# Third attention of a fused transformer tower: from steps of four token blocks and one head group to steps of two token blocks and both head groups

## The chip, the cores and the metric

The kernel runs on one core of one Trainium2 chip. The metric is the device time of one execution in microseconds (us), as the median of several runs; lower is better. A core has a matmul engine (TensorE, PE in the profile, with its weight loads shown apart as PEld), a vector engine (VectorE, DVE), an engine for activation functions (ScalarE, ACT), a general engine (GpSimd, POOL) and a queue that issues transfers (SyncE, SP). Each engine works through its own list of instructions in order; semaphores order the engines among each other.

## The reference, cut to what matters

The program is a small vision tower: a patch embedding, a feed-forward part, a windowed attention, a second attention with a cosine bias, and then a block whose attention is the third one here, followed by a mixture of eight experts. There are 16 images of 64 tokens each, with 64 features. The part that the change touches is this:

```python
h = _rmsnorm(x, ln1_w)
q = (h @ wq.T).reshape(Bx, Tx, NH, HD).transpose(0, 2, 1, 3)    # 4 heads of 16
k = (h @ wk.T).reshape(Bx, Tx, NKV, HD).transpose(0, 2, 1, 3)   # 2 heads, each for 2 query heads
v = (h @ wv.T).reshape(Bx, Tx, NKV, HD).transpose(0, 2, 1, 3)
q, k = q * cos + _rotate_half(q) * sin, k * cos + _rotate_half(k) * sin
scores = jnp.einsum('bhtd,bhsd->bhts', q, repeat(k)) / jnp.sqrt(jnp.float32(HD))
att = jax.nn.softmax(jnp.where(causal, scores, -1e30), axis=-1)
y = jnp.einsum('bhts,bhsd->bhtd', att, repeat(v)) ...
x = x + y @ wo.T
flat = _rmsnorm(x, ln2_w).reshape(-1, Cx)
...
for e in range(NE):                       # 8 experts, hidden width 170
    hh = jax.nn.silu(flat @ w1[e].T) * (flat @ w3[e].T)
    out = out + weights[:, e:e + 1] * (hh @ w2[e].T)
```

## The kernel before

The tokens of the 16 images are laid on two halves of the 128 partitions, which gives 512 columns. Every stage is worked in two halves of 256 columns, called g = 0 and g = 1. A block w (0 to 7) is one image of each partition half; a half g holds blocks 4g to 4g+3. The order of the work on each engine is written out by hand, so that an instruction waits both for its own semaphores and for all that stands ahead of it on its engine. Matmul results lie in eight PSUM banks of 512 columns (`PS[:, bank, column]`).

The third attention is done in four steps i = 0 to 3. A step i covers the half g = i // 2, all of its four blocks, and one of the two head groups (two heads each). It goes through these functions:

- `scores3(g)` on PE writes the scores of both steps of half g: 16 small matmuls, each of which the profile shows as 2 records (line L596). The first step's scores are in bank 4g, the second's in bank 4g+1. One semaphore increment by 2 at the end releases both steps. `open_scores3` has written the causal mask to all four banks before.
- `shift3(i)` on DVE takes the row maximum (`reduce_max`, L1234) and subtracts it (L1236), from 512 columns of PSUM to the tile `shifted`.
- `turn3(i)` on PE turns `shifted` in four transposes (L606).
- `probabilities3(i)` on ACT takes the exponential (L935).
- `mix3(i)` on PE multiplies by the values in 8 matmuls, 16 records (L620). The values are made by `values3(g)` on PE (L369) and copied by `values3(g)` on ACT (L928).

After the two steps of a half, `divide` on DVE (L1245 and L1247) normalises, `mixed_to_features` on PE turns back (L426), `attended_copy3` on ACT copies (L939), `open3` (L630) and `output3` (L635) on PE make the output projection with the residual, and `squares3` on ACT (L943), `sum_squares3` on DVE (L1409), a power on POOL (L1104), `high_part`, `normalised` and `low_part` on DVE (L1415, L1391, L1397) make the normalised features in two parts. `parts_to_features` on PE (L643) turns them, and `turned_copy` on ACT (L954) and on DVE (L1402) copy them to `xf`.

Then comes the loop over 22 chunks n of the experts' first products. For each n, PE does four matmuls of 512 columns (L707, L708), ACT a SiLU (L973), DVE a product (L1454). PE does `output3(1)`, the output projection of the second half of the third attention, between n = 0 and n = 1. From n = 3 on, the matmuls of n wait for the DVE product of n - 3.

The functions of ACT come in tables; `bring_table(func)` (L794) is a one-column activation that makes the load of a table (ACT_TABLE_LOAD) happen at a place of the program's choice. In the kernel before, the load for SiLU stands right behind `probabilities3(3)`, ahead of `turned_copy(0)` and `attended_copy3(1)`; copies can run with any table.

Of the kernel before, what the change touches and what calls it, by code (L numbers as in the profile page):

```python
# [26 lines left out]
P = 128  # L27
B, C, IMG, PATCH = 16, 3, 128, 16
GRID = IMG // PATCH
N = GRID * GRID  # L30
D = 64
HALF = 64
COLS = B * N * D // P
HC = COLS // 2
# [5 lines left out]
FH, FHD, FKV = 4, 16, 2  # L40
# [46 lines left out]
def build(nc, x0, x0_last, x1, pack_a, pack_b, pack_c, pack_d, pack_e, out):  # L87
    with ExitStack() as ctx:
# [5 lines left out]
        def sem(name):  # L94

            if name not in made:
                made[name] = ctx.enter_context(nc.semaphore(name))
            return made[name]

        idle_bf = sb("idle_bf", [P, 512], BF16)  # L100
        PS = ctx.enter_context(nc.psum_tensor("PS", [P, 8, 512], F32))
# [15 lines left out]
        def c(name):  # L117
            return Cp[:, columns(PACK_C, name)]
# [102 lines left out]
        def const(value):  # L221
            n = CONSTS.index(value)
            return consts[:, n:n + 1]
# [21 lines left out]
        def half(t, g):  # L245
            return t[:, g * HC:(g + 1) * HC]
# [53 lines left out]
        def _(pe):  # L300
            mm, tp = nc.tensor.matmul, nc.tensor.transpose
# [63 lines left out]
            def values(src, w, wide, bank, g):  # L365

                for u in (2 * g, 2 * g + 1):
                    at = (u % 2) * 2 * wide
                    t = mm(PS[:, bank, at:at + 2 * wide], src[:, u * P:(u + 1) * P], w, start=True, stop=True)  # L369
                return t  # L370
# [198 lines left out]
            def values3(g):  # L569
                values(h4f, c("fv"), FKV * FHD, 3 + 4 * g, g).then_inc(sem("v3_mm"), 1)  # L570
# [14 lines left out]
            turned_pair(1, ("fq", "fq_turned"))  # L585


            def scores3(g):

                pe.wait_ge(sem("q3_ready"), g + 1)  # L590
                pe.wait_ge(sem("k3_ready"), g + 1)
                for w in range(4 * g, 4 * g + 4):
                    for hg in range(2):
                        for s in range(2):
                            rows = slice(HALF * s + 32 * hg, HALF * s + 32 * hg + 32)
                            t = mm(PS[HALF * s:HALF * s + HALF, 4 * g + hg, (w % 4) * P:(w % 4 + 1) * P],  # L596
                                   q3[rows, w * N:(w + 1) * N], k3_heads[rows, w].rearrange("q h n -> q (h n)"),
                                   start=False, stop=True, skip_group_check=True)
                t.then_inc(sem("att3_scores"), 2)

            def turn3(i):
                if i >= 2:
                    pe.wait_ge(sem("att3_probs"), i - 1)
                pe.wait_ge(sem("att3_shifted"), i + 1)
                for n in range(4):
                    t = tp(PS[:, 2 + 4 * (i % 2), n * P:(n + 1) * P], shifted[:, i % 2, n * P:(n + 1) * P], ident)  # L606
                t.then_inc(sem("att3_turned"), 1)

            def mix3(i):
                g, ch = i // 2, i % 2  # L610
                if ch == 0:
                    pe.wait_ge(sem("v3_ready"), g + 1)
                pe.wait_ge(sem("att3_probs"), i + 1)
                wide = 2 * (FHD + 1)
                for k in range(2):
                    for s in range(2):
                        for p in range(2):
                            of, w = 2 * k + p, 4 * g + 2 * k + p
                            at = ((2 * k + s) * FKV + ch) * wide
                            t = mm(PS[HALF * p:HALF * p + HALF, 3 + 4 * g, at:at + wide],  # L620
                                   probs[:, i % 2, of * P + s * HALF:of * P + (s + 1) * HALF],
                                   vo3[:, p, (w // 2) * 2 + s, ch].rearrange("q e d -> q (e d)"), start=True, stop=True)
                t.then_inc(sem("att3_mixed"), 1)
# [15 lines left out]
            def parts_to_features(g):  # L639
# [4 lines left out]
                t.then_inc(sem("parts_turned"), 1)  # L644

            scores3(0)
            values3(0)
            values3(1)
            scores3(1)
            turn3(0)  # L650
            turn3(1)
            mix3(0)
            mix3(1)
            turn3(2)
# [32 lines left out]
            for n in range(2 * CH):  # L687
                g, ch = n // CH, n % CH
# [15 lines left out]
                for v in range(2):  # L704
                    at = (2 * ch + v) * P
# [83 lines left out]
        def _(act):  # L789
            f = nc.scalar.activation  # L790

            def bring_table(func):

                f(table_use[:, :], const(1.0), func)  # L794
# [91 lines left out]
            for g in range(2):  # L886
                act.wait_ge(sem("qk2_mm"), g + 1)
                for s in range(2):
                    r = slice(HALF * s, HALF * s + HALF)
                    t = f(q2[r, g * HC:(g + 1) * HC], PS[r, QK2_BANKS[s], 0:HC], ACT.Identity, scale=float(D) ** -0.5, bias=q2_bias[r, :])  # L890
# [9 lines left out]
            for g in range(2):  # L900
# [3 lines left out]
                at = slice(4 * g, 4 * g + 4)  # L904
# [7 lines left out]
            for g in range(2):  # L912
                act.wait_ge(sem("kr_ready"), g + 1)
                for h in range(2):
                    t = f(k3_heads[:, 4 * g:4 * g + 4, h, :], half(kr, g).rearrange("q (w n) -> q w n", n=N),
                          ACT.Copy, scale=c("fhead_mask")[:, h:h + 1])
# [14 lines left out]
            def probabilities3(i):  # L931
                act.wait_ge(sem("att3_turned"), i + 1)
                if i >= 2:
                    act.wait_ge(sem("att3_mixed"), i - 1)
                f(probs[:, i % 2, :], PS[:, 2 + 4 * (i % 2), :], ACT.Exp, scale=scale3).then_inc(sem("att3_probs"), 1)  # L935
# [5 lines left out]
            def squares3(g):  # L941
                act.wait_ge(sem("fo_mm"), g + 1)
                f(squares_eps[:, 4 * g:4 * g + 4, 0:D], PS[:, 4 * g, 0:HC].rearrange("q (t d) -> q t d", d=D), ACT.Square,  # L943
                  scale=float(D) ** -0.5).then_inc(sem("rms2_squared"), 1)
# [7 lines left out]
            def turned_copy(g):  # L952
                act.wait_ge(sem("parts_turned"), g + 1)
                f(xf[:, g, 1, :], PS[:, TURNED_BANKS[1][g], 0:HC], ACT.Copy).then_inc(sem("xf_ready1"), 1)  # L954
# [7 lines left out]
            attended_copy3(0)  # L962
            squares3(0)
            probabilities3(3)
            bring_table(ACT.Silu)
            turned_copy(0)
            attended_copy3(1)

            for n in range(2 * CH):
# [184 lines left out]
        def _(ve):  # L1154
# [27 lines left out]
            def scale(name, g, dst, src, by):  # L1182
                ts = slice(4 * g, 4 * g + 4)
                ve.wait_ge(sem(name + "_rstd"), g + 1)
                return v.tensor_tensor(tiles(dst)[:, ts], tiles(src)[:, ts], by[:, ts].unsqueeze(2).to_broadcast([P, 4, D]),
                                       ALU.mult)
# [41 lines left out]
            def shift(name, rows, n):  # L1228

                ve.wait_ge(sem(name + "_scores"), n + 1)  # L1230
                if n >= 2:
                    ve.wait_ge(sem(name + "_turned"), n - 1)
                tops = top[:, n % 2, :].rearrange("q (b h) -> q b h", b=2)
                v.reduce_max(tops, rows, AX).then_inc(sem(name + "_top"), 1)  # L1234
                ve.wait_ge(sem(name + "_top"), n + 1)
                v.tensor_tensor(shifted[:, n % 2, :].rearrange("q (b h n) -> q b h n", b=2, n=N), rows,  # L1236
                                tops.unsqueeze(3).to_broadcast([P, 2, 4, N]), ALU.subtract)\
                    .then_inc(sem(name + "_shifted"), 1)

            def divide(name, bank, g, heads, size):  # L1240

                ve.wait_ge(sem(name + "_mixed"), (4 if name == "att1" else 2) * (g + 1))
                mix = PS[:, bank, 0:4 * heads * (size + 1)].rearrange("q (w h d) -> q w h d", w=4, h=heads)
                rec = r1[:, 4 * g:4 * g + 4, 0:heads]
                v.reciprocal(rec, mix[:, :, :, size]).then_inc(sem(name + "_recip"), 1)  # L1245
                ve.wait_ge(sem(name + "_recip"), g + 1)
                v.tensor_tensor(on[:, 4 * g:4 * g + 4, :].rearrange("q w (h d) -> q w h d", h=heads), mix[:, :, :, 0:size],  # L1247
                                rec.unsqueeze(3).to_broadcast([P, 4, heads, size]), ALU.mult)\
                    .then_inc(sem(name + "_divided"), 1)
# [132 lines left out]
                v.tensor_tensor(half(kr, g), half(rope[:, 0], g), half(rope[:, 1], g), ALU.add).then_inc(sem("kr_ready"), 1)  # L1382
                rotate(g, 1).then_inc(sem("rope_q"), 1)
            def shift3(i):
                g, hg = i // 2, i % 2
                shift("att3", PS[:, 4 * g + hg, :].rearrange("q (b h n) -> q b h n", b=2, n=N), i)

            def normalised(g):
                ts = slice(4 * g, 4 * g + 4)
# [10 lines left out]
            def turned_copy(g):  # L1400
                ve.wait_ge(sem("parts_turned"), g + 1)
                v.tensor_copy(xf[:, g, 0, :], PS[:, TURNED_BANKS[0][g], 0:HC]).then_inc(sem("xf_ready0"), 1)  # L1402
# [16 lines left out]
            shift3(1)  # L1419
            shift3(2)  # L1420
            scale("ln1", 0, h4, sum2, rstd).then_inc(sem("h4_ready"), 1)
            scale("ln1", 1, h4, sum2, rstd).then_inc(sem("h4_ready"), 1)
            divide("att3", 3, 0, FH, FHD)
            shift3(3)
            sum_squares3(0)
            high_part(0)
# [23 lines left out]
            for n in range(2 * CH):  # L1450
                g, ch = n // CH, n % CH
# [56 lines left out]
                if n in (ROUTE_AT + 10, ROUTE_AT + 11):  # L1508
                    g = n - ROUTE_AT - 10
                    ts = slice(4 * g, 4 * g + 4)  # L1510
                    v.reduce_sum(means[:, ts], tiles(h45)[:, ts], AX).then_inc(sem("h45_step"), 1)
                if n in (ROUTE_AT + 12, ROUTE_AT + 13):
                    g = n - ROUTE_AT - 12
# [166 lines left out]
```

## Time and profile before

| what | value |
|---|---|
| median of 3 runs | 115.91 us (115.75 to 115.92) |
| the profiled execution, its device time | 115.73 us |
| its span, first to last recorded work | 113.9 us |
| PE busy | 100.1 us, 88% of the span |
| DVE busy | 81.2 us, 71% |
| ACT busy | 64.0 us, 56%, of it nine table loads, 11.5 us |
| third attention, scores to the last `turned_copy(0)` | about 59.6 to 72.4 us |
| loop over the experts' chunks | starts at 72.55 us |

A busy share is an average over stages. In a stage with a chain of dependent steps no engine is full, and the chain sets its time. A timeline row gives the start from the start of the span, the duration of the merged run of instructions, the engine, the line, what is written and read, and in brackets the idle time of that engine ahead of it and what ended that. The device time has 1.8 us more than the span.

### The profile page before, as it was taken

What the parts mean: (1) busy time and instruction counts of PE and PEld (TensorE: products, weight loads), DVE (VectorE), ACT (ScalarE), POOL (GpSimd) and SP (SyncE); (2) the same over time, 40 slices, a digit from 0 to 9 for tenths busy, and PEclk for the clock granted to TensorE, in tenths of its full rate; (3) what the DMA queues carried; (4) which work ended last, traced back from release to release, by engine and by line L of the source; (5) the groups of instructions that cost most, each with busy time, mean ns of one, the idle gap of its engine ahead of it and who ended that gap; (6) DMA issues with size and microseconds to landing.
All of it is one profiled execution on the core that took longest, in us unless ns stands there. A gap on an engine that the chain in (4) does not pass through costs nothing.

```text
span 113.9 us, 2196 instructions
## 1 busy us (share of the span) xinstructions
PE 100.1 (88%) x825; PEld 64.5 (57%) x828; DVE 81.2 (71%) x173; ACT 64.0 (56%) x125; POOL 33.3 (29%) x68
## 2 busy tenths in 40 slices
PE   5998979999999998977699887999999999999710
PEld 2334547376676764663568665688888874334400
DVE  0002417597889889889598975589589899976981
ACT  5005364976533754927388657467476667478040
POOL 7500034973830000000622073030012350879000
PEclk9999999999999999999999999999999999999985
DMA  3999994000000000000000000000000000000004
GB/s 125 368 387 419 441 409 172 0 0 0 6 0 0 0 3 6 3 0 0 0 0 6 0 0 6 0 0 0 0 0 6 3 0 0 3 0 0 0 0 92
DMA packets 2826, 6.99 MB, mean 61 GB/s; under 512 B 1280, under 2 KB 1408, under 8 KB 2688
## 3 DMA queue, kind: packets, MB, share of 16 engines
q1 hardware_dynamic: 2272, 6.72, 15.2%
q10 hardware_dynamic: 544, 0.13, 0.5%
q8 instruction: 6, 0.10, 0.4%
q14 instruction: 4, 0.03, 0.1%
HBM read 6.59 MB, written 0.26 MB: 60 GB/s over the span
## 4 chain that ended last, share of the span: by engine, by line
PE 59%; DVE 19%; ACT 7%; DMA 6%; issue 3%; SPq 2%; POOL 1%; DVEq 0%; ACTq 0%
PE PS L707 9%; PE PS L708 9%; PE PS L715 7%; DMA shared_x<-x_dram 6%; PE PS L393 4%; PE PS L351 4%; PE PS L575 3%; PE PS L404 3%; PE PS L361 3%; DVE shifted L1236 2%; DVE top L1234 2%; PE PS L418 2%; ACT shared_f L808 2%; PE PS L327 2%; PE PS L515 1%
## 5 line engine op out<-in xcount | busy, mean ns | idle before, releaser
L707 PE MATMUL PS<-xf,up_hi 128*128 128x512 f32 x44 | 17.8, 405 | 0.2 <-DVE xf L1402 0.2
L1454 DVE TENSOR_TENSOR shared_h<-PS,shared_f 128x512 f32<-128x512 f32 x22 | 15.0, 683 | 3.4 <-ACT shared_f L973 3.1
L708 PE MATMUL PS<-xf,up_lo 128*128 128x512 f32 x44 | 17.3, 394 | 0.0
L973 ACT ACTIVATE shared_f<-PS 128x512 f32<-128x512 f32 x22 | 13.1, 596 | 6.4 <-PE PS L708 6.2
L794 ACT ACT_TABLE_LOAD x9 | 11.5, 1283 | 0.9 <-PEq L1671 0.7
L1234 DVE TENSOR_REDUCE top<-PS 128x8 f32<-128x512 f32 x12 | 8.3, 688 | 3.0 <-PE PS L393 2.7
L707 PEld LDWEIGHTS PS<-xf,up_hi 128*128 128x128 f32 x44 | 8.3, 188 | 2.2 <-issue 0.4
L708 PEld LDWEIGHTS PS<-xf,up_lo 128*128 128x128 f32 x44 | 8.3, 188 | 1.8
L1236 DVE TENSOR_TENSOR shifted<-PS,top 128x512 f32<-128x512 f32 x12 | 8.3, 691 | 0.4
L867 ACT ACTIVATE probs<-PS 128x512 f32<-128x512 f32 x8 | 4.8, 598 | 5.6 <-PE PS L404 5.6
L808 ACT ACTIVATE shared_f<-PS,pack_b_sb 128x512 f32<-128x512 f32 x8 | 5.2, 685 | 4.7 <-PE PS L351 4.6
L715 PE MATMUL PS<-shared_h,down_w 128*64 128x512 f32 x32 | 7.7, 605 | 0.0
L1088 POOL TENSOR_SCALAR std<-sq_sums 128x8 f32<-128x8 f32 x1 | 0.2, 203 | 22.7 <-DVE sq_sums L1174 22.7
L327 PE MATMUL PS<-shared_x 128*64 128x256 f32 x48 | 6.7, 394 | 0.1
L309 PE MATMUL PS<-idle_bf 128*128 128x512 bf16 (+1 forms) x14 | 5.3, 488 | 1.5 <-POOL idle_bf L1016 1.3
L1530 DVE TENSOR_TENSOR shared_x<-PS,up_w 128x512 f32<-128x512 f32 x8 | 5.2, 686 | 1.5 <-PE PS L715 1.1
L1252 DVE TENSOR_SCALAR pos_b<-pack_a_sb 128x64 f32<-128x64 f32 x1 | 0.3, 253 | 8.2 <-DMA pack_a_sb<-pack_a_dram 8.2
L393 PE MATMUL PS<-shared_h,q_groups 64*128 64x256 f32 x32 | 5.6, 427 | 0.2 <-ACT shared_h L841 0.2
L999 ACT ACTIVATE up_w<-PS 128x512 f32<-128x512 f32 x8 | 4.2, 599 | 2.7 <-PE PS L729 2.7
L361 PE MATMUL PS<-shared_f,pack_b_sb 128*64 128x256 f32 x32 | 5.0, 405 | 0.6 <-ACT shared_f L808 0.6
L1142 POOL TENSOR_TENSOR shared_x<-shared_x 128x512 f32<-128x512 f32 x4 | 5.1, 1276 | 1.4 <-DVE shared_x L1530 1.4
L404 PE MATMUL PS<-pack_a_sb,shifted 128*128 128x128 f32 x32 | 5.2, 286 | 0.2 <-ACT q_groups L835 0.2
(206 smaller groups left out, 206.7 us busy)
## 6 DMA issues: line engine op xcount, KB each, us to landing
shared_x<-x_dram SPq DMA_DIRECT2D x3, 512.0 KB, 7.2
up_w<-pack_d_dram SPq DMA_DIRECT2D x1, 1408.0 KB, 11.2
shared_x<-x_dram SPq DMA_DIRECT2D x2, 576.0 KB, 4.0
pack_c_sb<-pack_c_dram SPq DMA_DIRECT2D x1, 796.5 KB, 12.7
shared_x<-x_last_dram SPq DMA_DIRECT2D x2, 288.0 KB, 5.4
pack_b_sb<-pack_b_dram SPq DMA_DIRECT2D x1, 455.0 KB, 8.5
down_w<-pack_e_dram SPq DMA_DIRECT2D x1, 352.0 KB, 13.1
pack_a_sb<-pack_a_dram SPq DMA_DIRECT2D x1, 162.0 KB, 5.6
```

The source lines that it names most:

```text
L327: m = mm(PS[HALF * s:HALF * s + HALF, 4 + g, 0:HC], weights, pixels, start=(n == 0 and k == 0), stop=(last and k == 1))
L361: t = mm(PS[r, bank, 0:HC], b("ff2")[:, m * D:(m + 1) * D], hidden[:, m, s, g * HC:(g + 1) * HC], start=(m == 0), stop=(m == 1))
L393: t = mm(PS[:, SCORE_BANKS[w % 2] + s, 0:HC], q_groups[r, w ^ s].rearrange("q h n -> q (h n)"), k_slots[r, w ^ s].rearrange("q h n -> q (h ...
L404: t = tp(PS[:, w % 2, ch * P:(ch + 1) * P], shifted[:, w % 2, ch * P:(ch + 1) * P], ident)
L707: mm(up, up_hi[:, at:at + P], moving, start=True, stop=False)
L708: mm(up, up_lo[:, at:at + P], moving, start=False, stop=True).then_inc(sem("up_mm"), 1)
L715: t = mm(PS[HALF * s:HALF * s + HALF, bank, tok], down_w[:, DOWN_AT[ch]:DOWN_AT[ch] + D], hh[:, ch, s, tok], start=True, stop=True)
L794: f(table_use[:, :], const(1.0), func)
L973: f(gate[:, n % UPBUF, :], PS[:, UP_BANKS[n % UPBUF][0], :], ACT.Silu).then_inc(sem("gated"), 1)
L1234: v.reduce_max(tops, rows, AX).then_inc(sem(name + "_top"), 1)
L1236: v.tensor_tensor(shifted[:, n % 2, :].rearrange("q (b h n) -> q b h n", b=2, n=N), rows, tops.unsqueeze(3).to_broadcast([P, 2, 4, N]), AL ...
L1454: v.tensor_tensor(hh[:, ch, :, g * HC:(g + 1) * HC], PS[:, UP_BANKS[n % UPBUF][1], :].rearrange("q (s c) -> q s c", s=2), gate[:, n % UPBU ...
```

## The change

Three things are changed.

1. A step i of the third attention is now half g = i // 2 and block pair k = i % 2 (two blocks) with both head groups. `scores3(i)` writes 8 matmuls for one step and releases that step alone. The banks are dealt anew: step (g, k) uses half of the columns of banks 4k and 4k+1. Steps 2 and 3 share banks with steps 0 and 1, in other columns, and `scores3` of these waits until the DVE has read step 0 or 1 (`att3_shifted`). `shift3` and `mix3` address accordingly; the shapes and the number of their instructions stay.
2. The written-out orders: on PE the scores of the four steps and the two `values3` are spread among the first two `turn3`; on DVE the second of the two `scale("ln1", ...)` stands behind `divide("att3", 3, 0, ...)` instead of ahead of it.
3. On ACT `turned_copy(0)` stands ahead of `bring_table(ACT.Silu)` instead of behind it.

```diff
-            def scores3(g):
-
+            def scores3(i):
+
+                g, k = i // 2, i % 2
+                if g == 1:
+                    pe.wait_ge(sem("att3_shifted"), k + 1)
                 pe.wait_ge(sem("q3_ready"), g + 1)
                 pe.wait_ge(sem("k3_ready"), g + 1)
-                for w in range(4 * g, 4 * g + 4):
+                for w in (4 * g + 2 * k, 4 * g + 2 * k + 1):
                     for hg in range(2):
                         for s in range(2):
                             rows = slice(HALF * s + 32 * hg, HALF * s + 32 * hg + 32)
-                            t = mm(PS[HALF * s:HALF * s + HALF, 4 * g + hg, (w % 4) * P:(w % 4 + 1) * P],
+                            at = g * HC + (w % 2) * P
+                            t = mm(PS[HALF * s:HALF * s + HALF, 4 * k + hg, at:at + P],
                                    q3[rows, w * N:(w + 1) * N], k3_heads[rows, w].rearrange("q h n -> q (h n)"),
                                    start=False, stop=True, skip_group_check=True)
-                t.then_inc(sem("att3_scores"), 2)
+                t.then_inc(sem("att3_scores"), 1)
...
             def mix3(i):
-                g, ch = i // 2, i % 2
-                if ch == 0:
+                g, k = i // 2, i % 2
+                if k == 0:
                     pe.wait_ge(sem("v3_ready"), g + 1)
                 pe.wait_ge(sem("att3_probs"), i + 1)
                 wide = 2 * (FHD + 1)
-                for k in range(2):
+                for ch in range(2):
                     for s in range(2):
                         for p in range(2):
-                            of, w = 2 * k + p, 4 * g + 2 * k + p
+                            of, w = 2 * ch + p, 4 * g + 2 * k + p
...
             scores3(0)
+            scores3(1)
             values3(0)
+            turn3(0)
+            scores3(2)
             values3(1)
-            scores3(1)
-            turn3(0)
             turn3(1)
+            scores3(3)
             mix3(0)
             mix3(1)
             turn3(2)
...
             probabilities3(3)
+            turned_copy(0)
             bring_table(ACT.Silu)
-            turned_copy(0)
             attended_copy3(1)
...
             def shift3(i):
-                g, hg = i // 2, i % 2
-                shift("att3", PS[:, 4 * g + hg, :].rearrange("q (b h n) -> q b h n", b=2, n=N), i)
+                g, k = i // 2, i % 2
+                shift("att3", PS[:, 4 * k:4 * k + 2, g * HC:(g + 1) * HC].rearrange("q b (h n) -> q b h n", n=N), i)
...
             scale("ln1", 0, h4, sum2, rstd).then_inc(sem("h4_ready"), 1)
+            divide("att3", 3, 0, FH, FHD)
             scale("ln1", 1, h4, sum2, rstd).then_inc(sem("h4_ready"), 1)
-            divide("att3", 3, 0, FH, FHD)
             shift3(3)
```

## Rows read from the trace of the kernel before

**Rows 1.** The page's busy times, share of the span and instructions of each engine.

```profile
PE 100.1 (88%) x825; PEld 64.5 (57%) x828; DVE 81.2 (71%) x173; ACT 64.0 (56%) x125; POOL 33.3 (29%) x68
```

**Rows 2.** The chain of waits in order of time: start us, us, what.

```profile
64.95 0.68 PE PS L620 x16
65.66 0.27 DVE r L1245
...
72.55 0.47 PE PS L707
```

**Rows 3.** Timeline of the attention's first half, 58.8 to 65.6 us.

```profile
58.87 1.28 ACT L794 ACT_TABLE_LOAD   x1
59.80 0.68 DVE L1375 TENSOR_TENSOR shared_f<-PS,pack_c_sb 128x512 f32<-128x512 f32 x1
...
60.67 1.10 PE L369 MATMUL PS<-pack_c_sb,h 128*128 128x64 f32 x8
60.81 0.69 DVE L1234 TENSOR_REDUCE top<-PS 128x8 f32<-128x512 f32 x1 [0.33 <-PE PS L596]
...
61.54 0.69 DVE L1236 TENSOR_TENSOR shifted<-PS,top 128x512 f32<-128x512 f32 x1
...
61.71 1.10 PE L596 MATMUL PS<-shared_x,qf 32*64 32x128 f32 x32
...
62.74 0.65 PE L606 MATMUL PS<-pack_a_sb,shifted 128*128 128x128 f32 x4
62.86 0.69 DVE L1236 TENSOR_TENSOR shifted<-PS,top 128x512 f32<-128x512 f32 x1
...
63.61 0.66 PE L606 MATMUL PS<-pack_a_sb,shifted 128*128 128x128 f32 x4 [0.21 <-DVE shifted L1236]
...
64.19 1.42 PE L620 MATMUL PS<-vo,probs 128*64 128x34 f32 x32
...
64.30 0.60 ACT L935 ACTIVATE probs<-PS 128x512 f32<-128x512 f32 x1 [0.27 <-PE PS L606]
...
64.84 0.75 DVE L1185 TENSOR_TENSOR h<-h,rstd 128x256 f32<-128x256 f32 x2
```

**Rows 4.** Timeline of its second half, 67.0 to 70.7 us.

```profile
67.01 0.69 DVE L1236 TENSOR_TENSOR shifted<-PS,top 128x512 f32<-128x512 f32 x1
...
67.34 0.71 PE L635 MATMUL PS<-pack_c_sb,attended 128*128 128x128 f32 x4
...
67.89 0.60 PE L606 MATMUL PS<-pack_a_sb,shifted 128*128 128x128 f32 x4
...
68.42 0.66 PE L620 MATMUL PS<-vo,probs 128*64 128x34 f32 x16
68.51 0.42 DVE L1409 TENSOR_REDUCE sq_sums<-squares_eps 128x4 f32<-128x260 f32 x1 [0.81 <-ACT squares_eps L943]
...
69.01 0.50 PE L630 MATMUL PS<-xf,ident_r 128*128 128x256 f32 x2
...
69.14 1.28 ACT L794 ACT_TABLE_LOAD   x1
...
70.44 0.20 ACT L794 ACTIVATE table_use<-consts 128x1 f32<-128x1 f32 x1
```

**Rows 5.** Timeline where the loop over the experts begins, 72.0 to 74.0 us.

```profile
72.02 0.38 ACT L954 ACTIVATE xf<-PS 128x256 fp32r<-128x256 f32 x1 [1.38 <-PE PS L643]
...
72.43 0.39 ACT L939 ACTIVATE attended<-PS 128x256 f32<-128x256 f32 x1
...
73.56 0.60 PE L635 MATMUL PS<-pack_c_sb,attended 128*128 128x128 f32 x4
...
73.92 0.48 PE L707 MATMUL PS<-xf,up_hi 128*128 128x512 f32 x1
```

**Rows 6.** Windows: stretch, its length, busy of each engine, granted PE clock, DMA.

```profile
54.00:56.00 2.00, 0.87 (x5) 0.59 (x5) 1.41 (x5) 1.05 (x3) 0.92 (x2) 1.00 0.00 0
...
84.00:94.00 10.00, 10.00 (x45) 7.98 (x44) 9.25 (x25) 6.68 (x14) 3.27 (x9) 1.00 0.01 2
```

## The prediction, made before the changed kernel was run

> **What bounds the kernel now.** I read the page's busy line first. PE is busy for 88% of the span [rows 1], and so it is the first suspect, but the share says nothing about a single stage. So I read the chain of waits next, for the stretch of the change. Between the scores and the start of the expert loop at 72.55 us the chain is not PE's alone. It passes from DVE to PE to ACT and back, and its joint is the first `divide`, at 65.66, which starts when the 16 records of `mix3(1)`, started at 64.95, are done [rows 2]. From `divide` to 72.55 everything follows step by step, 6.89 us. From there on PE is full: in 84 to 94 us it is busy for 10.00 of 10.00 us, while DVE has 9.25 and ACT 6.68 [rows 6]. So two questions decide. When does the first `divide` start, because what is won or lost there reaches the loop whole? And does PE, once in the loop, have to wait anywhere, because a full engine can't make up a wait?
>
> The timeline then gives the release of each step. In the first half DVE stands idle for 0.33 us ahead of its first maximum, for PE's scores; PE waits for 0.21 us ahead of `turn3(1)`, for DVE's shift [rows 3].
>
> **The first half: DVE starts earlier.** `shift3(0)` now needs 8 matmuls of scores in place of 16, so half of the time of the 32 records. The pitch of such a group is read from the second one, from its start at 61.71 to the start of the turn behind it at 62.74: 1.03 us, so 0.515 for 8 matmuls [rows 3]. The first scores are then done about half a microsecond before their old end, and DVE's rotation ahead of the shift, 59.80 plus 0.68, ends at 60.48 [rows 3]. DVE itself is the limit: `shift3(0)` starts at 60.48 instead of 60.81, and the 0.33 us of idle time are gone. The maximum and the subtraction keep their shape of 128 partitions by 512 elements; that they now read halves of two banks I cost at nothing, since they are still the same number of elements. The bounds: nothing, or 0.1 us for the four instructions of a step pair if two banks were slower. The shift of step 0 ends at 61.90 (before: 61.54 + 0.69 = 62.23), that of step 1 at 63.22 (before: 62.86 + 0.69 = 63.55) [rows 3]. If PE followed at once, all would be 0.33 us earlier.
>
> **PE does not follow.** Its new order is scores 0, scores 1, values 0, turn 0, scores 2, values 1, turn 1, scores 3, mix 0, mix 1. The pitches: a turn takes 0.58 (63.61 to 64.19); one `values3` half of the distance from 60.67 to 61.71, so 0.52 [rows 3]; a mix 0.59 (68.42 to 69.01) [rows 4], the last one 0.66 to its end, as there. `turn3(0)` waits for DVE and starts 0.05 after it, at 61.95 (before: 62.74, when it was held by scores 1). Then:
>
> - turn 0, scores 2 and values 1: 0.58 + 0.515 + 0.52 = 1.62, so `turn3(1)` starts at 63.57. DVE's shift would have let it go at 63.27. Lost: 0.30. So it goes 0.04 earlier than before.
> - turn 1, scores 3 and mix 0: 0.58 + 0.515 + 0.59 = 1.69, so `mix3(1)` starts at 65.26. The way over ACT (turn to exponential 0.69, the exponential 0.60, 0.05 to PE: 1.34, as from 63.61 to 64.95 [rows 2, 3]) would have let it go at 64.91. Lost here: 0.35.
>
> `scores3(3)` is the culprit of the second. Between `turn3(1)` and the end of its exponential PE has room for one mix and nothing else, and the scores of step 3 are not wanted by DVE until after `divide`. `mix3(1)` ends at 65.92 and `divide` starts at 65.95 to 65.97, against 65.66: the sum is -0.33 + 0.30 + 0.32 = **+0.29 us** (the 0.32 is the 0.35 less the slack of 0.03 in the handover to `divide`). The term's bounds: -0.33 if the moved groups cost PE nothing, and +0.6 if each group costs its whole shown duration (0.65, 0.55, 0.55, 0.66, 0.55, 0.66 and 0.66 make 4.28 from 61.95, so `divide` at about 66.28). I take +0.29, since the pitches are those of the same matmuls in the same engine state. The wait on `att3_shifted` that is added to scores 2 and 3 costs nothing: `turn3` of the same step stands ahead on PE and has already waited for it.
>
> **DVE's order.** The second `scale`, half of the 0.75 us at 64.84 [rows 3], is now behind `divide`. Before, it ran while DVE would have waited for `mix3(1)`. Now DVE has an idle stretch of nearly 1 us (its third shift ends at about 64.60, the first scale at about 64.98, `divide` starts at 65.95) and the scale comes after it. For `divide` it wins nothing, and the fourth shift goes 0.29 + 0.37 = 0.66 us later, from its end at 67.70 to about 68.36. What hides it: `sum_squares3(0)` on DVE is wanted at 68.51 + 0.29 = 68.80 [rows 4], 0.44 us after. The fourth turn, exponential and mix are late by 0.66 as well, and are followed by PE's idle time before `parts_to_features`, about 71.6. So 0, with 0.1 as the upper bound.
>
> From `divide` on, the chain's steps are the same ones in the same order: `turned_copy(0)` starts at 72.02 + 0.29 = 72.31, the loop at 72.84.
>
> **The table load.** Before, it starts at 69.14 and ends with its one-column activation at 70.64, so 1.50 us [rows 4]. All of it lies in time in which ACT waits: there are still 1.38 us of idle time ahead of the turned copy at 72.02 [rows 5]. With the late fourth step it would be at 69.8 to 71.3, still hidden, with 1.0 us to spare. Now `turned_copy(0)` stands ahead of it. The copy takes 0.38 (72.31 to 72.69), the load and its activation 1.50, and `attended_copy3(1)` starts at 74.21 instead of 72.43 and ends at 74.60 instead of 72.82 [rows 5]. Who waits for that? `output3(1)`, which stands on PE between n = 0 and n = 1 of the loop. It ran from 73.56 [rows 5], and without the load it could run at 73.85. Now it starts at 74.65, 0.05 after the copy: PE stands for 0.80 us. Behind such a wait the matmuls that follow start 0.55 us after it, as from 67.34 to 67.89 [rows 4], and not 0.36 as in the running pipeline, 73.56 to 73.92 [rows 5]: 0.19 more. Together **+0.99 us**. The loop's chunk n = 1 starts at 75.20 instead of 73.92. The first SiLU starts at about 74.6 and its product on DVE is done at about 75.9, before PE wants it for n = 3 at about 77.1, so no second wait follows. Bounds: 0.80 without the refill, 1.2 if the first SiLU or the squares of the second half then hold something. In the loop PE has no idle time [rows 6], and all of the 0.99 stays.
>
> The trace shows no time between the load's end at 70.42 and its activation at 70.44 [rows 4]. The Trainium skill, ScalarE: Activation LUTs, section What ACT_TABLE_LOAD costs, gives a drain of about 1.38 us on top of the load's 1.28, 2.66 us for every switch. The row disagrees about the drain: 1.50 with the activation. By the page's price PE would stand for about 1.2 us more, and the time would be near 118.4.
>
> **The sum.** +0.29 + 0.99 = +1.28 us. Against the profiled execution that is a span of 115.2 and a time of 115.73 + 1.28 = 117.0. The median of the runs shown is 115.91, 0.18 above the profiled one, so that I give 115.91 + 1.28 = **117.2 us**. A measurement of this kernel can tell about 0.2% (0.23 us) from no change, and the forecast is five times that.
>
> **The rivals.**
>
> - *PE's moved groups do overlap.* If scores and values run beside the turns, the 0.33 us of DVE's earlier start comes through and only the table load costs: -0.33 + 0.99 = +0.66, 116.6 us. For it: the score matmuls use only 32 rows by 64 columns of the array, and 32 records of them pass in 1.03 us. Against it: this overlap among themselves is already in the pitch of 0.515 [rows 3].
> - *The load is off the path, and the time goes to faster.* The place is ACT between its last exponential, about 69.8, and the turned copy at 72.3: if the load ran ahead of the waiting copy, it would be hidden as now. Its 0.99 falls away. From there the attention's term alone decides: faster if it is below zero, down to -0.33 and 115.6 us; at my value +0.29 and 116.2. Against it: the load at 58.87 [rows 3] comes in the order of the program, behind the copies of the first half's keys, which any table serves; nothing ran it ahead of them. It is the only way to a gain, because the bounds of the attention's term alone can't pay for the 0.99.
> - *The PE clock falls after the new stall.* The granted clock has two levels, 1.2 and 2.4 GHz, and it is 1.00 (2.4) throughout this part. A stall of 0.8 us follows a thin stretch. If the clock then fell to the lower level in the loop, each microsecond of matmuls at it would cost up to one more, 118 us and above. Against it: from 54 to 56 PE is busy for only 0.87 of 2.00 us and the clock stays at 1.00 [rows 6].
> - *The load costs more than the row*, by a drain or by a late first SiLU: 1.5 to 2.2 us in place of 0.99, so 117.8 to 118.4.
>
> **How the numbers follow.** The forecast has 0.77, the overlap 0.11, the load off the path 0.05 (0.02 with a gain, 0.01 near zero, 0.02 slower), the clock 0.03, the dearer load 0.04. So faster 0.02, same 0.02, slower 0.96. The range is 116.5 to 117.8: down to the overlap case at 116.6, up to the attention's upper bound and the load's upper bound together (0.6 + 1.2). It leaves out some 0.13 at both ends.
>
> **What the changed profile would show.** The first maximum of the third attention at about 60.48 with no idle time ahead of it; `turn3(0)` at about 61.95; `turn3(1)` close to its old time with no wait for DVE; L620 as two groups without a gap, and `divide` with nearly 1 us of idle time ahead of it, at about 65.95; the SiLU table load at about 72.7 instead of 69.1; `output3(1)` with idle time of about 0.8 us released by `attended_copy3(1)`; chunk n = 1 of the loop 1.28 us later, and that distance kept to the end. The prediction is wrong if `divide` starts before 65.66, if the load stands ahead of the turned copy, or if the loop's later part is not full and takes the stall up.

## The result, and the profile after

The changed kernel takes 116.94 us (median of 5 runs, 116.70 to 117.43) against 115.92 us for the kernel before (5 runs, 115.75 to 116.50). The ratio is 1.0077 with a 95% interval of 1.0041 to 1.0113, so it is slower by 0.5 to 1.3 us. The forecast was 117.2, in a range of 116.5 to 117.8, and slower. Timed once more, beside other kernels, it gave 1.0084 (1.0055 to 1.0112).

The profiled execution took 116.81 us with a span of 115.0 us. Start times are not quite comparable between executions, because the head of the program lasts differently long in each (no run says why): in the thirteen traces of this study A, below, lies between 59.69 and 61.40 us, though the code ahead of it is the same. The 61.40 us belong to the kernel with the values first, whose profiled execution was a slow one, 1.2 us above that kernel's median, with all of the excess ahead of A. So I measure from one fixed place, the start of DVE's last rotation ahead of the attention (L1375 before, L1381 after), and call it A.

| from A to ... | before | after | difference |
|---|---|---|---|
| A itself, from the start of the span | 59.80 | 59.88 | +0.08 |
| first `divide` | 5.86 | 6.05 | +0.19 |
| `turned_copy(0)` | 12.22 | 12.42 | +0.20 |
| turn of the routes, ahead of the last chunk's end | 34.20 | 35.18 | +0.98 |
| last normalisation | 51.37 | 52.35 | +0.98 |

Everything arises in two places, 0.20 us in the attention and 0.79 between the first two chunks of the loop (2.16 us from n = 0 to n = 1, 72.83 to 74.99, against 1.37, 72.55 to 73.92), and what is lost stays lost. First, the timeline of the attention after the change, the answer to [rows 3]; lines of the code have moved by 4 to 6 (L600 was L596, L610 was L606, L624 was L620, L1240 was L1234):

```profile
59.88 0.68 DVE L1381 TENSOR_TENSOR shared_f<-PS,pack_c_sb 128x512 f32<-128x512 f32 x1
...
60.48 0.68 DVE L1240 TENSOR_REDUCE top<-PS 128x8 f32<-128x512 f32 x1
...
61.95 0.65 PE L610 MATMUL PS<-pack_a_sb,shifted 128*128 128x128 f32 x4 [0.52 <-DVE shifted L1242]
...
62.53 0.67 PE L600 MATMUL PS<-shared_x,qf 32*64 32x128 f32 x16
...
63.13 0.66 PE L369 MATMUL PS<-pack_c_sb,h 128*128 128x64 f32 x4
63.27 0.69 DVE L1240 TENSOR_REDUCE top<-PS 128x8 f32<-128x512 f32 x1
...
63.62 0.61 PE L610 MATMUL PS<-pack_a_sb,shifted 128*128 128x128 f32 x4
...
64.16 0.67 PE L600 MATMUL PS<-shared_x,qf 32*64 32x128 f32 x16
...
64.76 1.13 PE L624 MATMUL PS<-vo,probs 128*64 128x34 f32 x32
...
65.93 0.26 DVE L1251 RECIPROCAL r<-PS 128x16 f32<-128x16 f32 x1 [0.92 <-PE PS L624]
...
67.61 0.69 DVE L1242 TENSOR_TENSOR shifted<-PS,top 128x512 f32<-128x512 f32 x1
...
68.78 0.42 DVE L1415 TENSOR_REDUCE sq_sums<-squares_eps 128x4 f32<-128x260 f32 x1 [0.47 <-ACT squares_eps L949]
```

The reader is to see three things. DVE's first maximum has no idle time ahead of it any more. From 61.95 on PE has no idle time up to the end of both mixes (L624): the second turn is not released by DVE, as in [rows 3], it starts when the values ahead of it are through. And the wait has moved to DVE: 0.92 us ahead of `divide`, released by PE. The fourth shift ends at 68.30, 0.47 us ahead of the sum of squares that is wanted.

Then the start of the loop, the answer to [rows 5] and to the table load in [rows 4]:

```profile
72.30 0.38 ACT L960 ACTIVATE xf<-PS 128x256 fp32r<-128x256 f32 x1 [2.59 <-PE PS L647]
...
72.70 1.28 ACT L800 ACT_TABLE_LOAD   x1
...
72.83 0.47 PE L713 MATMUL PS<-xf,up_hi 128*128 128x512 f32 x1 [0.16 <-DVE xf L1408]
...
73.99 0.20 ACT L800 ACTIVATE table_use<-consts 128x1 f32<-128x1 f32 x1
74.10 0.37 ACT L945 ACTIVATE attended<-PS 128x256 f32<-128x256 f32 x1
74.37 0.59 ACT L979 ACTIVATE shared_f<-PS 128x512 f32<-128x512 f32 x1
...
74.52 0.71 PE L639 MATMUL PS<-pack_c_sb,attended 128*128 128x128 f32 x4 [0.52 <-ACT attended L945]
...
74.99 0.48 PE L713 MATMUL PS<-xf,up_hi 128*128 128x512 f32 x1
```

ACT now has 2.59 us of idle time ahead of the turned copy, room enough for the load (1.28) that stands behind it. `output3(1)` (L639) starts 1.69 us after the loop's first matmul, where it started 1.01 after it before [rows 2, 5]. The idle time in the bracket, 0.52, is less than the 0.68 us of delay, because the last matmul ahead of it is drawn to its modelled end; the distance of the starts is the safer number.

The window of the full loop is as before [rows 6], PE busy 10.00 of 10.00 us at a granted clock of 1.00:

```profile
84.00:94.00 10.00, 10.00 (x45) 8.03 (x44) 9.19 (x26) 6.68 (x14) 2.53 (x8) 1.00 0.01 2
```

### The profile page after: what moved, and what is told of

Its sections match the earlier page's. It is cut to its first block, busy times and chain, and to the rows that moved or that the text cites. A ratio compares the mean times of both kernels' runs of the same rounds, so it can differ in the third digit from the quotient of the medians.

```text
span 115.0 us, 2201 instructions
## 1 busy us (share of the span) xinstructions
PE 101.0 (88%) x828; PEld 64.3 (56%) x828; DVE 81.2 (71%) x173; ACT 63.8 (55%) x125; POOL 33.3 (29%) x68
## 4 chain that ended last, share of the span: by engine, by line
PE 60%; DVE 18%; ACT 9%; DMA 5%; issue 3%; SPq 1%; POOL 1%; ACTq 0%; DVEq 0%
PE PS L713 9%; PE PS L714 8%; PE PS L721 7%; DMA shared_x<-x_last_dram 5%; PE PS L393 4%; PE PS L351 4%; PE PS L327 3%; PE PS L404 3%; PE PS L361 3%; PE PS L575 3%; ACT shared_f L814 2%; PE PS L418 2%; DVE shifted L1242 2%; DVE top L1240 2%; PE PS L639 1%
## 5 line engine op out<-in xcount | busy, mean ns | idle before, releaser
L1460 DVE TENSOR_TENSOR shared_h<-PS,shared_f 128x512 f32<-128x512 f32 x22 | 15.0, 683 | 4.2 <-ACT shared_f L979 3.9
L1240 DVE TENSOR_REDUCE top<-PS 128x8 f32<-128x512 f32 x12 | 8.2, 687 | 2.8 <-PE PS L393 2.7
L309 PE MATMUL PS<-idle_bf 128*128 128x512 bf16 (+1 forms) x16 | 5.9, 478 | 1.3 <-POOL idle_bf L1022 1.3
```

The lines of the kernel that those rows point to most:

```text
L1460: v.tensor_tensor(hh[:, ch, :, g * HC:(g + 1) * HC], PS[:, UP_BANKS[n % UPBUF][1], :].rearrange("q (s c) -> q s c", s=2), gate[:, n % UPBU ...
```

## The experiments

My theory: two costs that add up, the order on PE (about 0.2 us) and the table load (about 0.8 us), each passed on whole. The rivals: that one of them is harmless; that the loop takes up a stall; that other edits (DVE's order) have a part. All comparisons are against the kernel before on the same chip. The interval of the timed ratios is 0.24 to 0.45% (0.3 to 0.5 us) to each side, so that for terms of 0.1 to 0.4 us the distances inside the traces carry the verdict, and the ratio is only a coarse test of them. Each run has one trace; how well the distances repeat is seen where a kernel was run twice. The two traces of the changed kernel have 52.35 and 52.37 us from A to the end, those of the reordered one 50.95 twice.

| kernel | ratio (95%) | A to divide | A to turned copy | A to last normalisation |
|---|---|---|---|---|
| before | 1 | 5.86 | 12.22 | 51.37 |
| changed | 1.0077 (1.0041 to 1.0113) | 6.05 | 12.42 | 52.35 |
| load back | 1.0009 (0.9983 to 1.0035) | 6.05 | 12.41 | 51.55 |
| load alone | 1.0048 (1.0019 to 1.0078) | 5.87 | 12.23 | 52.18 |
| scale back too | 1.0009 (0.9980 to 1.0038) | 6.05 | 12.41 | 51.56 |
| scores of step 3 late | 1.0007 (0.9981 to 1.0034) | 5.74 | 12.52 | 51.69 |
| values first | 0.9998 (0.9974 to 1.0022) | 5.75 | 12.12 | 51.27 |
| load last | 1.0039 (1.0015 to 1.0062) | 6.04 | 12.41 | 51.71 |
| two more loads | 1.0508 (1.0477 to 1.0539) | 6.04 | 12.41 | 57.69 |
| two more loads, PE kept busy | 1.0321 (1.0276 to 1.0365) | 6.04 | 12.41 | 55.36 |
| reordered | 0.9995 (0.9970 to 1.0020) | 5.44 | 11.81 | 50.95 |
| reordered, again | 0.9937 (0.9912 to 0.9963) | 5.43 | 11.80 | 50.95 |

**The load back.** The changed kernel with

```diff
             probabilities3(3)
-            turned_copy(0)
             bring_table(ACT.Silu)
+            turned_copy(0)
             attended_copy3(1)
```

> The changed kernel with the SiLU table load back ahead of the turned copy. My theory: the load costs 0.79 us (from the two traces, n = 0 to n = 1 of the loop takes 2.16 us instead of 1.37) and nothing else follows from it, so the time is 0.2 to 0.3 us above the kernel before, about 116.2. In the trace output3(1) has no idle time for the attended copy, and divide stays at about 65.9. Rival (the load is harmless, the cost is in the attention): the time stays near 116.9.

Measured: ratio 1.0009, and 0.18 us more than before from A to the end. The attention's part is the same as in the changed kernel to 0.01 us, the load's 0.79 to 0.80 us are gone. The timeline shows the load hidden, with 1.07 us still to spare, although it starts later behind the late fourth step:

```profile
70.16 1.28 ACT L800 ACT_TABLE_LOAD   x1
...
71.45 0.20 ACT L800 ACTIVATE table_use<-consts 128x1 f32<-128x1 f32 x1
...
72.72 0.38 ACT L960 ACTIVATE xf<-PS 128x256 fp32r<-128x256 f32 x1 [1.07 <-PE PS L647]
```

**The load alone.** The kernel before with only the ACT edit.

> The kernel before with only the table load moved behind the turned copy. My theory: 0.8 us slower than before, about 116.7, with the whole distance arising between n = 0 and n = 1 of the loop and kept to the end. Rival (the stall is taken up later in the loop): no slower than 0.2 us.

Measured: ratio 1.0048, and 0.81 us from A to the end (51.37 to 52.18), all of it behind the turned copy, which stands at 12.23 as before. `output3(1)` (L635 here) starts 1.69 us after the loop's first matmul (73.30), as in the changed kernel:

```profile
74.58 0.37 ACT L939 ACTIVATE attended<-PS 128x256 f32<-128x256 f32 x1
...
74.99 0.71 PE L635 MATMUL PS<-pack_c_sb,attended 128*128 128x128 f32 x4 [0.52 <-ACT attended L939]
```

The two parts add up: 0.81 + 0.18 = 0.99 against 0.98 for both. The rival that the loop takes the stall up is out.

**The scale back too.** As the first, with DVE's `scale` and `divide` in the order of before.

> As the first, and the second scale of DVE back ahead of divide. My theory: the scale ran and runs in idle time, so this differs from the first by less than 0.1 us; the fourth shift ends about 0.35 us earlier in the trace. Rival (the late fourth shift costs): 0.3 us faster than the first.

Measured: the same as the first to 0.01 us in each phase. The fourth shift's subtraction started 0.34 us earlier (7.39 instead of 7.73 us after A), and the fourth turn (8.28 instead of 8.57) and the table load with it, but all of that ends in waits: the turned copy and the end did not move. The edit on DVE costs and brings nothing, as costed.

**The scores of step 3 late.** The changed kernel with the load back and

```diff
             turn3(1)
-            scores3(3)
             mix3(0)
             mix3(1)
+            scores3(3)
             turn3(2)
```

> As the first, and the scores of step 3 on PE moved from ahead of the first two mixes to behind them. My theory: PE's queue held mix3(1), so divide starts about 0.3 us earlier, 65.6; but the scores now stand ahead of turn3(2) and mixed_to_features, which takes 0.2 us of it back: 0.05 to 0.15 us faster than the first. Rival (divide waits for the exponential or DVE, not for PE's queue): divide does not move.

Measured: the ratio tells nothing (1.0007), the trace tells more. `divide` comes 0.31 us earlier, so that PE's queue held it, as I had said. But the turned copy comes 0.11 us later than in the first, and the end 0.14: I had expected a small gain. The rows name what took it:

```profile
66.13 0.67 PE L600 MATMUL PS<-shared_x,qf 32*64 32x128 f32 x16
...
66.73 0.66 PE L610 MATMUL PS<-pack_a_sb,shifted 128*128 128x128 f32 x4
...
67.22 0.38 PE L426 MATMUL PS<-pack_a_sb,s 128*128 128x128 f32 x2
...
67.42 0.60 ACT L941 ACTIVATE probs<-PS 128x512 f32<-128x512 f32 x1 [0.91 <-PE PS L610]
...
67.92 0.38 ACT L945 ACTIVATE attended<-PS 128x256 f32<-128x256 f32 x1
```

The scores push `turn3(2)` back (it starts 6.22 us after A, with the load back alone 5.93), that pushes the third exponential (L941) back (6.91 against 6.62), and this stands ahead of `attended_copy3(0)` (L945) on ACT, which starts at 7.41 instead of 7.29. `mixed_to_features` (L426) itself is 0.11 us earlier (6.71 against 6.82), so it is not what holds the copy; it starts at 67.92, 0.10 ahead of the exponential's reported end, as neighbours on ACT do here. I had counted only PE's queue behind the moved group and had left ACT's out.

**The values first.** The changed kernel with the load back and `values3(1)` ahead of `turn3(0)`.

> The changed kernel with the table load back, and the second values product on PE moved ahead of turn3(0), into PE's idle time there. My theory: turn3(1) starts with the second shift, at about 63.25 instead of 63.6, the first divide 0.35 us earlier, about 65.6, and the time equals that of the kernel before within 0.1 us or is up to 0.1 faster. Rival (the matmuls are not what holds turn3(1)): no change against the kernel with the load back, 0.2 to 0.3 us above before.

Measured: `divide` 0.30 us earlier than with the load back alone, and this time the turned copy (12.12) and the end (51.27) keep it: 0.28 us better than the first, 0.10 better than before. Its profile gives the turn at its release:

```profile
64.06 0.67 PE L600 MATMUL PS<-shared_x,qf 32*64 32x128 f32 x16
64.79 0.66 PE L610 MATMUL PS<-pack_a_sb,shifted 128*128 128x128 f32 x4
```

The turn starts 3.39 us after A (61.40) instead of 3.74. The matmuls of values had held it; the rival is out. The two traces of the reordered kernel below, which has this edit too, have the turn at 3.39 and 3.38. The 12.12 and 51.27 rest on this one trace; the timed ratio, 0.9998 (0.9974 to 1.0022), can't tell 0.1 us.

**The load last.** The changed kernel with the load behind `attended_copy3(1)`, so that only the SiLU waits for it.

> The changed kernel with the table load one place later still, behind the attended copy, so that only the SiLU waits for it. My theory: it is output3(1), waiting for the attended copy, that stalls PE, and the SiLU has slack of more than 1 us until n = 3 of the loop wants its product, so PE doesn't stall there and the time is that of the kernel with the load back, 0.2 to 0.3 us above before, though the load is still not hidden from ACT. Rival (any unhidden load delays the loop): 0.8 us more, as the changed kernel.

Measured: 51.71, which is 0.64 us better than the changed kernel, and 0.16 worse than with the load back. The main point holds: `output3(1)` starts 1.01 us after the loop's first matmul again, and PE does not stall there, though the load is not hidden from ACT. So it is the attended copy behind the load that stalls PE, not the load as such. The 0.16 I had not expected. The starts of PE's matmuls are the same to 0.01 us as with the load back until `parts_to_features(1)` (L647), which waits for DVE's residual (L1411):

```profile
75.87 1.28 DVE L1460 TENSOR_TENSOR shared_h<-PS,shared_f 128x512 f32<-128x512 f32 x2
...
76.03 1.01 POOL L1110 TENSOR_TENSOR rstd_rms<-sq_sums,minus_half 128x4 f32<-128x4 f32 x1 [5.93 <-DVE sq_sums L1415]
...
77.07 0.42 DVE L1397 TENSOR_TENSOR normed<-PS,rstd_rms 128x256 f32<-128x256 f32 x1
...
78.34 0.42 DVE L1411 TENSOR_TENSOR attended<-PS,h 128x256 f32<-128x256 f32 x1
...
78.82 0.66 PE L647 MATMUL PS<-pack_a_sb,parts 128*128 128x128 f32 x4
```

The residual comes 6.24 us after the turned copy, with the load back 6.08, and PE's next chunk 6.60 us after the loop's first matmul instead of 6.47: 0.13 of the 0.16. DVE is late by the same 0.16 already at the normalisation (L1397, 4.97 us after the turned copy instead of 4.81). Two things end together just ahead of it, and this trace doesn't tell which one holds it: the products of the late SiLUs, which DVE does back to back here (L1460, to 77.15, and a successor on DVE starts about 0.08 us ahead of the reported end), and POOL's power (L1110, to 77.04), which is late because the squares of the second half stand behind the late first SiLU on ACT, and their sum behind its product on DVE. With the load back the power had ended 0.7 us ahead of the normalisation. No further run tests it. So the loop has a second place, six chunks in, where a late ACT reaches PE.

**Two more loads.** The changed kernel with a switch to the exponential's table and back behind the first (the second argument of `bring_table` is a column of `table_use`, which is three columns wide here).

```diff
             turned_copy(0)
             bring_table(ACT.Silu)
+            bring_table(ACT.Exp, 1)
+            bring_table(ACT.Silu, 2)
             attended_copy3(1)
```

> The changed kernel with two more table switches (exponential and back to SiLU) behind the first one. My theory: the stall of PE is passed on whole, so two further loads with their activations of 1.50 us each, less some overlap of neighbours, make it 2.8 to 3.0 us slower than the changed kernel, about 119.8. Rival (a part of a stall is taken up in the loop): clearly less than 2.8. If the clock falls in the longer stall, more than 3.0, and the granted clock shows it.

Measured: ratio 1.0508, and 5.34 us more than the changed kernel from A to the end, not 3.0. `output3(1)` is 3.01 us later after the loop's first matmul (4.70 instead of 1.69), as expected for two loads. The other 2.3 us come behind it, and the windows show with what. Columns are the window, its length, busy time of PE, PEld, DVE, ACT and POOL, granted clock, DMA:

```profile
74.00:76.00 2.00, 0.00 (x0) 0.00 (x0) 0.00 (x0) 1.98 (x4) 0.00 (x0) 0.90 0.00 0
76.00:78.00 2.00, 0.65 (x3) 0.66 (x4) 0.19 (x1) 1.77 (x4) 0.00 (x0) 0.50 0.00 0
78.00:80.00 2.00, 2.00 (x7) 1.69 (x7) 0.93 (x2) 0.92 (x2) 0.47 (x1) 0.50 0.00 0
80.00:82.00 2.00, 2.00 (x6) 1.53 (x5) 0.69 (x1) 0.66 (x2) 0.54 (x1) 0.50 0.00 0
82.00:84.00 2.00, 2.00 (x9) 1.60 (x9) 1.64 (x4) 1.23 (x3) 0.00 (x0) 0.89 0.00 0
```

**PE kept busy.** The same kernel with 16 idle matmuls on PE ahead of `output3(1)`, that is, matmuls whose results nobody reads.

```diff
                 if n == 1:
+                    stay_awake(16, 1)
                     output3(1)
```

> The kernel with two more table switches, and 16 idle matmuls on PE (512 columns, about 0.22 us each, into a bank that the next chunk overwrites) in the long stall ahead of output3(1). The two more switches made it 5.1 us slower than the changed kernel, 3.0 of them in the stall itself. My theory: the other 2.3 us is the PE clock, which its trace shows at 0.50 after 3.5 us without a matmul; with the idle matmuls it stays at 1.00 and the kernel is only 3.0 us slower than the changed one, about 119.9. Rival (something else in the loop is held by the late ACT): still 5 us slower.

Measured: ratio 1.0321, 55.36 from A to the end, 3.01 us more than the changed kernel. `output3(1)` again starts 4.70 us after the loop's first matmul, so the stall itself is the same; the 2.3 us behind it are gone and the clock stays up:

```profile
74.00:76.00 2.00, 2.00 (x9) 1.06 (x10) 0.14 (x1) 1.98 (x3) 0.00 (x0) 1.00 0.00 0
76.00:78.00 2.00, 2.00 (x11) 0.92 (x10) 0.00 (x0) 1.98 (x3) 0.00 (x0) 1.00 0.00 0
```

So the clock was the 2.3 us, and the two loads cost what they delay, 3.01 us, with nothing taken up later.

**Reordered.** The load back, both values products ahead of `turn3(0)`, the scores of step 3 behind the mixes, and, against the trap that the late scores had shown, the third turn and the third exponential behind the first half's output:

```diff
             scores3(1)
             values3(0)
+            values3(1)
             turn3(0)
             scores3(2)
-            values3(1)
             turn3(1)
-            scores3(3)
             mix3(0)
             mix3(1)
-            turn3(2)
+            scores3(3)
             mixed_to_features("att3", 3, 0)
             open3(0)
             output3(0)
+            turn3(2)
...
-            probabilities3(2)
             attended_copy3(0)
             squares3(0)
+            probabilities3(2)
             probabilities3(3)
```

> A version meant to beat both: table load back, both values products ahead of turn3(0), scores of step 3 behind the first two mixes, turn3(2) behind output3(0), and on ACT the third exponential behind the squares. My theory: divide at about 65.25, output3(0) at about 66.95 instead of 67.34 before, the loop 0.4 us earlier than in the kernel before: 115.5. Rival (the late third and fourth step now end last): the loop waits for the second half's projection, and the time is that of the kernel before or more.

> The reordered version once more, since its trace shows 0.42 us gained between the attention's start and the end while its timed ratio was 0.9995 with 0.0025 to each side. My theory: 0.3 to 0.4 us faster than before (ratio about 0.9965). Rival (the gain isn't there in the time): ratio 1.000 or above.

> The changed kernel itself once more, beside the others on one chip. The traces say 0.98 us from the attention's start to the end, so a ratio of about 1.0085; within the noise seen so far, 1.006 to 1.011.

Measured: both traces of it give 50.95 from A to the end, 0.42 us better than before, and these rows of its timeline show each piece going at its release (A is 60.48 here):

```profile
63.87 0.66 PE L610 MATMUL PS<-pack_a_sb,shifted 128*128 128x128 f32 x4
...
64.45 1.42 PE L624 MATMUL PS<-vo,probs 128*64 128x34 f32 x32
...
65.92 0.26 DVE L1251 RECIPROCAL r<-PS 128x16 f32<-128x16 f32 x1 [0.31 <-PE PS L624]
```

The two timed ratios are 0.9995 (0.9970 to 1.0020) and 0.9937 (0.9912 to 0.9963). Their intervals don't overlap, and no run says why; 0.42 us would be a ratio of 0.9964, which lies between the two and just outside both. That it is faster than before is shown by the distances of two traces and by one of the two timings; how much faster in device time stays open. The changed kernel, timed beside the second of them, had 1.0084 (1.0055 to 1.0112), as expected.

## Why the prediction was right, by its own steps

- **DVE starts earlier, -0.33.** Right, a little small. The first maximum comes 0.60 us after A instead of 1.01, so 0.41. I took DVE's next instruction to start at the reported end of the one before; it starts 0.08 us ahead of it.
- **Maximum and subtraction over two banks at nothing.** Right: 0.68 to 0.69 us each, and 0.71 to 0.73 from start to start, before and after.
- **PE does not follow, +0.30 and +0.32.** Right in both places. `turn3(1)` went 3.74 us after A, DVE's shift was done at 3.33, so a loss of 0.35 after the same handover. The second place cost 0.26: from `turn3(1)` to `divide` it is 2.31 us, before 2.05. That is 0.61 in all, forecast 0.62. The pitches used were 0.58, 0.515 and 0.52, the measured ones 0.58, 0.60 and 0.49 in the first place, and 0.54 and 0.60 for the turn and the scores of the second: a group of 8 score matmuls behind a turn takes 0.60, while half of a group of 16 takes 0.515. So the three groups of the first place took 1.67 instead of 1.615, the two of the second 1.14 instead of 1.095, and the two mixes gave this back with 1.13 instead of 1.25. That these errors of the sizes cancel is luck. The sum from the first turn to the end of the second mix was forecast as 3.97 and came out as 3.94 (61.95 to 65.89). The two experiments on PE's order show both places: each of them moved one group and brought `divide` forward by 0.30 or 0.31 us. The net cost of the attention is +0.20, forecast +0.29, and the difference is the 0.08 on DVE.
- **DVE's order at 0.** Right, shown by the kernel with the scale back.
- **The table load, +0.99.** The mechanism was right and the size was 0.79. The attended copy came 1.80 us after the turned copy, before 0.41, so the load cost ACT 1.39 and not 1.50: the short activation of L800 is followed by the next one after 0.11 us, not after its 0.20. PE's delay was 0.68 instead of 0.80, and the refill behind it (0.47 to the next chunk's matmul against 0.36) cost 0.11 instead of 0.19, the 0.55 having been taken from a turn and not from a chunk of the loop.
- **The rule on the drain.** The row decided rightly: the load's end at 73.98 is followed by its activation at 73.99, and two more loads cost 3.01 us together. The 2.66 us for each switch that the Trainium skill gives (ScalarE: Activation LUTs, What ACT_TABLE_LOAD costs) are in no trace here.
- **Passed on whole.** Right for the stall of the changed kernel (0.98 us at the route turn and at the end). It isn't a law of this loop: in the load-last kernel the first SiLU waits for the load as well, and PE loses only 0.16.
- **The rivals.** The overlap of PE's groups did not come. The load did not run ahead: it started at the end of the turned copy. The clock stayed at 1.00 in the changed kernel's loop, with a stall of 0.68 us; the rival's mechanism is real, though, and the kernel with two more loads shows it and its price.
- **The sum.** +1.28 forecast, +1.08 in the profiled executions (115.73 to 116.81) and +0.98 from A on. Two small slips stand in the forecast's numbers: the range's upper end adds up to 117.7 (115.91 + 0.6 + 1.2), not 117.8, and the chances by case give slower 0.97 and same 0.01, where the last line has 0.96 and 0.02.

## What to carry to other kernels

An instruction that frees one engine earlier brings something only if the next engine's written-out queue has room at that moment: count, for each release, what stands between it and the instruction that it releases, on every engine of the chain. The reordered kernel won 0.42 us in its traces with the same step size that had lost 0.20, by moving only work whose consumer is late. (No run has the old steps with a better order, so how much of the 0.42 the smaller steps bring isn't shown.) A fixed cost like a table load belongs in a wait that exists already; if it must stand elsewhere, put it behind the last result that the full engine wants soon: that cut its cost here from 0.80 us to 0.16.

## What the runs showed of the hardware that was not expected

- The longer stall cost more than its length. In the kernel with two more loads PE, without a matmul from 73.80 on, kept its granted clock for a while (1.00 in 74.0 to 75.5, 0.62 in 75.5 to 76.0), and then stood at 0.50, the lower of its two levels of 1.2 and 2.4 GHz. It stayed there after the matmuls began again at 77.35, through the windows to 82 (0.89 in 82 to 84, 1.00 in 84 to 94), and this cost 2.3 us beyond the 3.0 of the longer stall. In the changed kernel, with PE's delay of 0.68 us, the clock stayed at 1.00 (72.83 to 84). The Trainium skill has the same two levels and a return to the lower one after idling (TensorE: Matmul & The Clock Gate, What's actually happening), and the traces agree. 16 idle matmuls filled 3.63 us of the wait and kept the clock at 1.00.
- Small activations follow each other faster than they last: 0.11 us from start to start for a row of 0.20 (73.99 to 74.10 in the changed kernel), and on DVE a successor that has nothing to wait for starts 0.08 us ahead of the reported end (60.48 against 59.88 + 0.68). Together these two put the forecast off by 0.08 us in the attention and 0.11 at the load.
- The spread of this kernel's time lies for a good part in its head: A came at 59.69 to 60.97 us in the twelve traces other than that of the values first, with the same code ahead of it, while in the seven of them with PE's order of the changed kernel the time from A to the turned copy was 12.41 or 12.42.
